# Routing of the second expert layer moved into the second attention, batch by batch, with a third projection bank

## The reference, cut to what matters

```python
logits = xf @ router_w.T                  # xf: normalised tokens, 2048 x 512; router_w: 8 x 512
topk_vals, topk_idx = top_k(logits, 2)
topk_w = softmax(topk_vals)
order = argsort(topk_idx.reshape(-1))     # every token goes to its two experts
x_sorted = xf[order // 2]
```

## Time and profile before

| | us |
|---|---|
| median of 3 runs | 3307.08 (3305.06 to 3311.99) |
| the profiled execution, its own time | 3308.09 |
| its span from first to last instruction | 3305.9 |
| layer1_attention up to the last `final` | 2064.9 to 2853.5 |
| from the last `final` to the first instruction of layer1_experts | 2853.5 to 2987.0 |
| layer1_experts and the copy | 2987.0 to 3305.9 |

### The profile page before, as it was taken

The page is one execution under the profiler, slowest core; times in us unless marked ns, Lnnn a source line. Parts: engine busy times, 40 slices in busy tenths (PEclk is TensorE's granted clock), DMA queues, the critical chain, the costliest instruction groups (busy, mean ns, idle before and its releaser), DMA issues. The chain is left out here.

```text
span 3305.9 us, 57383 instructions
## 1 busy us (share of the span) xinstructions
PE 2887.7 (87%) x16324; PEld 1656.1 (50%) x16325; DVE 1797.5 (54%) x5172; ACT 1695.5 (51%) x4502; POOL 1740.7 (53%) x2429
## 2 busy tenths in 40 slices
PE   4699999999999969999999997699899999634996
PEld 2366666666666635555555543344444444322663
DVE  3366656656666555343433444588888887321331
ACT  5577777777777623223332333466666666311332
POOL 6467766776677435345544543655555655241222
PEclk9899999999999989999999998899999999757998
DMA  6601100010011055445544565355545555327444
GB/s 239 223 27 36 49 29 29 35 51 29 29 35 45 30 192 155 134 134 160 153 135 133 159 183 134 74 107 106 108 105 109 109 104 106 101 84 273 85 83 105
DMA packets 459854, 348.33 MB, mean 105 GB/s; under 512 B 295728, under 2 KB 366512, under 8 KB 459696
## 3 DMA queue, kind: packets, MB, share of 16 engines
q1 hardware_dynamic: 396896, 267.79, 29.0%
q0 software_dynamic: 16640, 38.05, 5.7%
q10 hardware_dynamic: 46224, 41.36, 4.2%
HBM read 194.88 MB, written 93.50 MB: 87 GB/s over the span
## 5 line engine op out<-in xcount | busy, mean ns | idle before, releaser
L437 PE MATMUL a_mm<-a_w_hi,a_xq_hi 128*128 128x512 f16 x768 | 301.9, 393 | 65.2 <-POOL a_xq_lo L885 61.5
L1646 POOL TENSOR_TENSOR e_st<-e_st,e_ws_tile 128x1024 f32<-128x1024 f32 x64 | 123.7, 1933 | 429.8 <-PE e_y L1402 418.9
L601 DVE BATCH_NORM_STATS2 a_st<-a_mm 128x6 f32<-128x128 f32 x768 | 170.7, 284 | 326.1 <-PE a_mm L438 231.6
L750 ACT ACTIVATE a_nrm<-a_mm,a_sc_t 128x128 f32<-128x128 f32 x768 | 290.4, 472 | 106.3 <-POOL a_sc_t L903 106.1
L438 PE MATMUL a_mm<-a_w_hi,a_xq_lo 128*128 128x512 f16 x768 | 303.2, 395 | 0.0
L1440 ACT ACTIVATE e_hh<-e_ha 128x512 f16<-128x512 f32 x128 | 76.3, 596 | 415.8 <-PE e_ha L1387 414.4
L1535 DVE SCALAR_TENSOR_TENSOR e_hl<-e_ha,e_hh 128x512 f16<-128x512 f32 x128 | 88.4, 691 | 352.3 <-ACT e_hh L1440 351.8
L902 POOL TENSOR_TENSOR a_sc_t<-a_sc_t,a_mhalf 128x4 f32<-128x4 f32 x192 | 202.5, 1055 | 138.3 <-DVE a_sc_t L608 138.0
L1811 PE MATMUL a_mm<-l_wh,a_src_hi 128*128 128x512 f16 x512 | 200.1, 391 | 76.0 <-DVE a_vl L1893 41.7
L1400 PE MATMUL e_y<-e_w2h,e_hh 128*128 128x512 f16 x640 | 242.6, 379 | 0.0
L1401 PE MATMUL e_y<-e_w2l,e_hh 128*128 128x512 f16 x640 | 242.6, 379 | 0.0
(11 more groups left out here) (350 smaller groups left out, 8294.6 us busy)
## 6 DMA issues: line engine op xcount, KB each, us to landing
e_st<-in_w SPq DMA_DIRECT2D x128, 512.0 KB, 4.3
disp<-a_empty SPq DMA_DIRECT2D x16, 781.5 KB, 4.1
e_st<-in_w1b SPq DMA_DIRECT2D x32, 352.0 KB, 3.1
e_xb<-disp ACTq DMA_DIRECT2D x41, 260.5 KB
disp<-a_empty SPq DMA_DIRECT2D x4, 2605.0 KB, 21.5
e_xb<-disp SPq DMA_DIRECT2D x40, 260.5 KB, 4.4
a_cx<-in_ctxT SPq DMA_DIRECT2D x32, 256.0 KB, 3.2
a_stage<-in_wprojT SPq DMA_DIRECT2D x16, 512.0 KB, 4.8
```

Source lines behind the costliest of these rows:

```text
L437: pe.matmul(out, xq_hi[:, n, c, :], w_hi[:, t, c, :], start=(c == 0), stop=False)
L750: ins = act.activation(nrm[:, n % 2, i * P:(i + 1) * P], src[:, i * P:(i + 1) * P], ACT.Identity, bias=sc_t[:, n % 2, 3, i:i + 1], scale=s ...
```

## The change

The stage `norm_route` goes. Its work is done in `layer1_attention` for one batch at a time, by new stages `r_*` at the end of the batch. Each expert now has room for all 2,048 rows (`disp1` holds 8 x 2,048 rows and one empty block), so a row's place is known at once: the expert's start, the rows counted so far, and the prefix within the batch. At the end of the attention a table `row_of_tile` is made, from which `layer1_experts` reads where each of its 40 tiles begins. The eight projections use three PSUM banks in turn in place of two, and the routing has a bank of its own. `c_high` and `c_low` move from slot 6 to the head of slot 2. Two loops of batches are unrolled at the start in place of one.

```diff
-FILL = 3
+FILL = E
+PAD = E * T
...
+HEAD1 = 2
+BANK1 = [t % MM_BANKS for t in range(NJ1)]
+BEFORE1 = [max(u for u in range(-NJ1, t) if BANK1[u % NJ1] == BANK1[t]) for t in range(NJ1)]
...
-        MMB = [s.ps(f"mm{n}", [P, DM]) for n in range(2)]
+        MMB = [s.ps(f"mm{n}", [P, DM]) for n in range(MM_BANKS)]
+        RB = s.ps("rb", [P, DM])
...
-            run_pipeline(pe, [("job", 0, project), ("att", 0, scores),
-                              ("att", 5, pv), ("att", 6, out_project)], NJ1, SCORE1, None, 2)
+            run_pipeline(pe, [("end", 10, r_transpose), ("end", 11, r_logits), ("end", 13, r_prefix), ("job", 0, project), ("att", 0, scores),
+                              ("att", 5, pv), ("att", 6, out_project)], NJ1, SCORE1, None, 2, HEAD1)
...
+            def r_transpose(b, k, q):
...
+                pe.wait_ge(sem["r_norm"], b + 1)
+                for c in range(KT):
+                    mm = pe.transpose(RB[:, c * P:(c + 1) * P], xr[:, c * P:(c + 1) * P], ident[:])
+            def r_logits(b, k, q):
+                pe.wait_ge(sem["r_t"], b + 1)
+                for c in range(KT):
+                    mm = pe.matmul(RB[:, 0:E], xrT[:, c * P:(c + 1) * P], wg[:, c, :], start=(c == 0), stop=(c == KT - 1))
+            def r_prefix(b, k, q):
+                pe.wait_ge(sem["r_mask"], b + 1)
...
+                pe.matmul(RB[:, 0:E], up16[:, 0, :], rm[:, 0, :], start=True, stop=False)
+                pe.matmul(RB[:, 0:E], up16[:, 1, :], rm[:, 1, :], start=False, stop=True).then_inc(sem["r_px"], 1)
...
+            def r_scores(b, k, q):
+                dve.wait_ge(sem["r_lgt"], b + 1)
+                dve.tensor_copy(rlg, RB[:, 0:E]).then_inc(sem["r_lg"], 1)
+                dve.wait_ge(sem["r_lg"], b + 1)
+                ch.add(dve.tensor_reduce(rnb, rlg, AX_X, ALU.max, negate=True))
+                ch.link(dve.max(rtop, rlg))
+                dve.max_index(rix[:], rtop, rlg).then_inc(sem["r_top"], 1)
...
+            def r_inverse(b, k, q):
+                dve.wait_ge(sem["r_exp"], b + 1)
+                ch.add(dve.tensor_scalar(xr[:, DM:DM + 1], trash[:, bass.ds(b, 1)], -float(TRASH), 0.5, ALU.add, ALU.mult))
+                dve.reciprocal(rinv, rsum).then_inc(sem["r_rinv"], 1)
...
-                               ("end", 7, final), ("in", 3, x_stats)], NJ1, SCORE1, ch, 2)
+                               ("end", 7, final), ("end", 7, r_stats), ("in", 3, x_stats), ("end", 11, r_scores), ("end", 12, r_inverse),
+                               ("end", 13, r_slots)], NJ1, SCORE1, ch, 2, HEAD1)
...
-            run_pipeline(act, [("att", 2, p_high),
+            run_pipeline(act, [("in", 2, c_high), ("att", 2, p_high),
...
-                               ("in", 6, c_high)], NJ1, SCORE1, None, 2)
+                               ("end", 9, r_norm), ("end", 10, r_keep), ("end", 12, r_exp), ("end", 13, r_gates)],
+                         NJ1, SCORE1, None, 2, HEAD1)
...
-            run_pipeline(pool, [("job", 0, scales), ("in", 3, x_scale), ("in", 5, tables), ("in", 6, c_low)],
-                         NJ1, SCORE1, ch, 2)
+            run_pipeline(pool, [("in", 2, c_low), ("job", 0, scales), ("in", 3, x_scale), ("in", 5, tables), ("end", 8, r_scale),
+                                ("end", 14, r_scatter)], NJ1, SCORE1, ch, 2, HEAD1)
+            pool.wait_ge(scattered, 2 * 32 * B)
...
             def load(i, q):
-                act.dma_start(xb[:, q, :], disp[bass.ds(i * P, P), :]).then_inc(x_in[q], 16)
+                at = act.value_load(row_of_tile[0:1, bass.ds(i, 1)], min_val=0, max_val=PAD)
+                act.dma_start(xb[:, q, :], disp[bass.ds(at, P), :]).then_inc(x_in[q], 16)
...
-        norm_route(nc, I, tokens(x4), disp1, expert_of_tile, tile_oh, scattered)
```

More of the change, by code:

```diff
@@ L147, in slot @@
                 continue
-            for late in range(3):
+            for late in range(4):
                 u = t + late * jobs - off
@@ L941, in _ @@
             pool.wait_ge(scattered, 32 * B)
[L945 to L967, removed]
@@ L1725, in layer1_attention @@
             "vhi", "vlo", "score", "max", "exp", "rinv", "phi", "plo", "turning", "pv", "ohi", "olo", "proj", "xres",
-            "x3", "out")}
+            "x3", "out", "rconst", "r_first", "r_stat", "r_scal", "r_norm", "r_tr", "r_t", "r_lgt", "r_lg", "r_top",
+            "r_exp", "r_rinv", "r_gate", "r_mask", "r_px", "r_pos", "r_slot", "r_sum", "r_cnt")}
         x_turned = [s.sem(f"x_turned_{n}") for n in ("h", "l")]
@@ new lines, in r_inverse, with r_slots @@
+            def r_inverse(b, k, q):
+                dve.wait_ge(sem["r_exp"], b + 1)
+                ch.add(dve.tensor_scalar(xr[:, DM:DM + 1], trash[:, bass.ds(b, 1)], -float(TRASH), 0.5, ALU.add, ALU.mult))
+                dve.reciprocal(rinv, rsum).then_inc(sem["r_rinv"], 1)
+            def r_slots(b, k, q):
+                dve.wait_ge(sem["r_px"], b + 1)
+                for n in range(2):
+                    ins = dve.scalar_tensor_tensor(out=rhit, in0=iota_e, scalar=rbest[:, n:n + 1], in1=RB[:, 0:E],
+                                                   op0=ALU.is_equal, op1=ALU.mult, accum_out=rslot[:, n:n + 1])
+                    ch.link(ins) if n == 0 else ins.then_inc(sem["r_pos"], 1)
+                dve.wait_ge(sem["r_pos"], b + 1)
+                dve.tensor_copy(sidx[:], rslot).then_inc(sem["r_slot"], 1)
@@ new lines, in _ @@
+            tt, ts = dve.tensor_tensor, dve.tensor_scalar
+            start, count, whole, jump = (seg[:, n, :] for n in range(4))
+            ch.link(ts(count[:, 0:E], iota_e, -float(T), None, ALU.mult))
+            dve.wait_ge(sem["r_cnt"], 1)
+            ch.link(tt(count[:, 0:E], RB[:, E:2 * E], count[:, 0:E], ALU.add))
+            ch.link(ts(count[:, 0:E], count[:, 0:E], 1.0 / P, (P - 1.0) / P - 0.5 + 0.5 / P, ALU.mult, ALU.add))
+            ch.link(ts(whole[:, 0:E], count[:, 0:E], 1.5 * 2.0 ** 23, 1.5 * 2.0 ** 23, ALU.add, ALU.subtract))
@@ new lines, in _ @@
+            ch.link(dve.memset(start[:, 0:1], 0.0))
+            ch.link(ts(jump[:, 0:E], whole[:, 0:E], -float(P), float(T), ALU.mult, ALU.add))
+            for e in range(E):
+                ch.link(tt(start[:, e + 1:e + 2], start[:, e:e + 1], whole[:, e:e + 1], ALU.add))
+            ch.link(tt(te[:], tile_no.unsqueeze(2).to_broadcast([P, TILES, E]),
+                       start[:, 1:E + 1].unsqueeze(1).to_broadcast([P, TILES, E]), ALU.is_ge))
+            ch.link(dve.tensor_reduce(tef[:, 0, :], te[:, :, 0:E - 1], AX_X, ALU.add))
```

310 lines of the change are left out of this document (115 added, 195 removed).

## The result

The changed kernel takes 3333.39 us (median of 4 runs, 3331.61 to 3338.55), the kernel before 3309.53 in the same comparison. The ratio is 1.0077, with a 95% interval of 1.0063 to 1.0091: slower by some 24 us. The forecast was 3317 with a range of 3240 to 3358, slower with a chance of 0.52.

What follows compares the result with a forecast made beforehand. No single engine was taken as the bound: PE and the chain DVE, ACT, DVE take turns. The terms summed as 3308.1 - 112.8 + 114.4 + 9 - 1.0 = 3317.7, stated as 3317 us, range 3240 to 3358.

Steps and rivals of the forecast that it cites:

- What goes: Stretch from the last `final` to the experts: 133.4 us less a remaining tail of 20.6, so 112.8 us saved.
- The last two batches: End of layer 1's attention, no projections left: they grow by DVE terms alone, 4.4 us each, +9 us.
- The experts: Expert stage: value_load stands with a load started a tile ahead, so it costs 0.
- The period: `final` to `final` in layer 1's attention: a batch grows by 8.8 us, from 46.8 to 55.6.
- third bank: Layer 1's projections: removes PE's wait for v_low, 2.4 us a batch at most, but was credited with nothing.
- context split: Slot 2: c_high waits for its load and delays p_high, c_low delays scales; +1.9 us a batch.
- r_norm, transposes and clock: Ahead of slot 6's projection: PE waits for r_norm and does four transposes, +2.3 us, plus +1.4 for clock, each batch.
- of it the clock: PE in layer 1's attention: half clock behind idle stretches costs +1.4 us a batch.
- r_exp and r_inverse: End of a batch: DVE waits for two exponentials on ACT, two hand-overs and a reciprocal; +1.2 us a batch.
- A: Rival for the attention batch: waits take up the new work, growth 3.4 us, 3247.5 us, faster; chance 0.27.
- B: Rival for the attention batch: the added work disappears, growth below 2.5 us, 3203 to 3236 us; chance 0.09.
- C: Rival: late slots 2 and 6 halve the clock, DVE waits for projections; growth 11 to 15 us, 3346 to 3398; chance 0.14.

Runs made afterwards that it cites:

- e4: The changed kernel with layer 1's projections on two PSUM banks in turn instead of three: 3317.9 us.
- e11: The kernel before, with c_high and c_low moved to the head of slot 2 and two loops unrolled at the start: 3345.4 us.
- e3: The changed kernel with c_high and c_low put back in slot 6: 3317.9 us.
- e1: The changed kernel with PE's four transposes moved from ahead of slot 6's projection to behind it: 3283.1 us.
- e6: e1 with c_high and c_low also put back in slot 6: 3281.4 us.
- e5: The changed kernel with 20 extra matmuls on PE ahead of the transposes' wait, their result overwritten: 3307.8 us.
- e9: The changed kernel with transposes behind slot 6's projection, two banks, and r_inverse one slot later on DVE: 3265.1 us.
- e12: The kernel before, with three banks for layer 1's projections and nothing else changed: 3303.7 us.

## Why the prediction was right, and where it was off

The sign, the main mechanism and the size by the range were right: the change trades 113 us of a stretch at 0.51 clock for a longer period, and the balance turns at 8 us a batch. The number was 16 us low. It was in part luck: the sign had a chance of 0.52, the sum lay 0.8 us a batch above the balance, and the terms of the period were right only together, as the table below shows. Of the signs named for the profile after, ACT's stall for `a_cx`, the scales behind c_low and the clock of 0.92 came true; the period (56.7, not 55 to 56), PE's wait for `a_xr` (5.6, not 2 to 3) and the start of the experts (18.3 us behind the last `final`, not 20 to 21) didn't.

- *What goes*: 112.8 expected, 115.1 measured.
- *The last two batches*: 9 expected, 11.1 measured. *The start*: 0 with a bound of -3; -2.3.
- *The experts*: 0 expected, +3.1 measured. From the first tile's `e_yb` to the last are 242.6 us and before 242.4, so the value_load is hidden; what was added lies ahead of the first `e_yb` (50.4 us into the stage, before 47.1), and its cause wasn't tested.
- *The fill* cost nothing: layer 0's experts begin at 1173.7, before it was 1177.4, and the fills of 2084 KB land in a median of 7.8 us.
- *The period*: 8.8 expected, 9.9 measured, and this is where most of the 16 us come from (1.1 x 13 = 14).

Within the period, the step that failed is "I give it nothing, since the DVE and ACT chain that makes v_low late stays, and PE would only reach the wait for r_norm sooner". Both halves of that sentence came true; what it missed is that reaching the wait sooner has a price. The third bank turned two waits of 2.3 and 2.6 us into one of 5.6, and the clock fell to half behind it in each of the ten batches, where e4 has that in four of ten: +1.4 us a batch. Without the third bank the growth was 8.5 us, against my 8.8, and the time 3317.9, against 3317.

That agreement isn't one of each term. Taken one by one:

| term | expected | measured |
|---|---|---|
| context split | 1.9 | 2.4 alone (e11), 1.0 in the change (e3), about 0 in e1 (e6; 1.2 at the same clock) |
| r_norm, transposes and clock | 3.7 | 3.8 come back with the transposes behind the projection (e1) |
| of it the clock | 1.4 | 2.0 (e5) |
| r_exp and r_inverse | 1.2 | 0.25 come back with r_inverse a slot later (e9) |
| third bank | 0 | +1.4 in the change (e4), -0.1 alone (e12) |

The walk added up stalls as if each were paid in full. They are not independent: what the split back gives is lost again to the clock on e1, and DVE's wait for r_exp comes back at the next hand-over. r_stats and r_scores weren't tried by themselves. The wait at the transposes was expected at 2 to 3 us a batch and was 5.6. I had taken the distance from pv's end to o_high's start from the kernel before, where the two met within a few tenths at 2431.26; in the changed kernel PE is there 4.5 us earlier.

Of the rivals, A (the waits take it up) fell: DVE's new work is about the 3.4 us that A took (3.6 by the estimate above, 1.9 in its busy time), the period grew by 9.9, and DVE's share went down from 84% to 72%. B fell with it. C's mechanism, the half clock in two places of a batch, is there, but only 2.0 us of it reach the period, and PE didn't come to wait for DVE at every projection.

## What to carry to other kernels

In a schedule with engines in order, what a new wait costs is read from the lead that the waiting engine has at that place and from what stands behind it in its list: the same four transposes cost 3.8 us a batch more ahead of a projection that DVE needs than behind it, and two short DMAs that issue from a half idle POOL cost 3.8 us a batch where they stood ahead of the scales. Another buffer ahead of a wait that ends at a fixed time doesn't shorten the waiting but gathers it in one piece, and on TensorE one long piece can cost more than two short ones. The mean clock of a stage doesn't tell what the half clock costs; compare batches with and without it at the place where others wait for PE. Price stalls by trying them together: their sum was near the truth here, and hardly any single term was.

## What the runs showed of the hardware

After 5.9 us without a matmul PE came back at 1.2 GHz and stayed there for nine of a projection's twelve matmuls (0.63 us for a matmul of 512 columns, 0.38 otherwise); 20 matmuls without use in that gap brought ten batches from a clock of 0.92 to 0.99 and saved 25.6 us. In e4, with a mean gap of 2.3 us at the same place and 2.6 at another, the clock was 0.95. In e1 a batch at 0.83 behind the transposes took 53.6 to 54.0 us and one at 1.00 took 52.0 to 52.1. The same DVE groups took 554 and 753 ns in the mean in the change and 611 and 924 with only the context split moved (e3). An indirect DMA of 128 rows keeps POOL for 1.1 and 0.98 us, 2.4 with the pause between the two.
